# A graph network on one core: row-tiled second table, even edge loads, a wider record row, block numbers turned by PE, a fourth buffer for hop chunks

## What is computed

```python
# layer 0: basis message, self term, rows normalised
agg = segment_sum(h[src] @ W_msg + b_msg, dst);  out = agg + h @ W_self + b_self;  x += out / max(norm(out), 1e-12)
# layer 1: one of 16 relation matrices per edge
x += segment_sum(h[src] @ W_rel[edge_type], dst)
# layer 2: three hops over the weighted adjacency
emb = acc = h
for _ in range(3):
    emb = segment_sum(edge_weight[:, None] * emb[src], dst);  acc = acc + emb
x += acc / 4
# layer 3: an edge network with a gate
hidden = leaky(leaky(concat(xs[src], xt[dst], edge_attr @ We.T + be) @ W1.T + b1) @ W2.T + b2)
x += segment_sum(relu(hidden @ W3.T + b3) * xs[src], dst) + xt
```

## Time and profile before

| what | us |
|---|---|
| median of three runs | 8440.53 |
| the profiled execution | 8453.61 |
| its span | 8451.6 |
| PE busy | 5784.8 |
| DVE busy | 4682.9 |
| POOL busy | 4978.6 |
| ACT busy | 1528.8 |

### The profile page before, as it was taken

How to read it: one execution, slowest core, us unless ns; L and a number is a source line. 1 busy time by engine, 2 the same in 40 slices (tenths; PEclk the granted TensorE clock), 3 DMA queues, 4 the chain that set the end, 5 groups by cost and what they waited for, 6 DMA issues and landing times.

```text
span 8451.6 us, 133532 instructions
## 1 busy us (share of the span) xinstructions
PE 5784.8 (68%) x42197; PEld 4230.0 (50%) x42197; DVE 4682.9 (55%) x10280; ACT 1528.8 (18%) x4330; POOL 4978.6 (59%) x5265
## 2 busy tenths in 40 slices
PE   2476777777776555556554477777767788778877
PEld 2466666666644555555554222222235555555555
DVE  3688898998863667667664200000025555555555
ACT  1111111111122111111110000000013333333333
POOL 0577777777733777777777411111117777777776
PEclk6566556555555666666665699999976656665666
DMA  5655555555543444444442599999953333333332
GB/s 135 97 92 89 89 93 91 92 93 89 90 101 106 71 68 71 68 69 69 68 71 42 201 426 401 423 426 397 426 217 87 82 82 82 81 82 82 82 81 69
DMA packets 794607, 1178.96 MB, mean 139 GB/s; under 512 B 619664, under 2 KB 647729, under 8 KB 766544
## 3 DMA queue, kind: packets, MB, share of 16 engines
q1 hardware_dynamic: 616460, 919.49, 35.5%
q0 software_dynamic: 172528, 250.20, 16.2%
q10 hardware_dynamic: 5204, 4.11, 0.2%
HBM read 921.76 MB, written 258.23 MB: 140 GB/s over the span
## 4 chain that ended last, share of the span: by engine, by line
POOL 45%; issue 20%; DMA 16%; PE 12%; DVE 5%; ACTq 1%; DVEq 1%; POOLq 0%; ACT 0%; SPq 0%
POOL arena L497 44%; DMA arena<-B_d 12%; PE ps L931 5%; DMA arena<-tab,idx 2%; PE ps L842 2%; PE ps L884 2%; DVE ps L1228 1%; ACTq L279 1%; DMA arena<-rec_d,tcol 1%; DVE arena L1231 1%; DVE pair L1204 1%; PE ps L871 1%; PE ps L835 1%; DVE arena L1229 1%; POOL recb L506 1%
## 5 line engine op out<-in xcount | busy, mean ns | idle before, releaser
L497 POOL DMA_INDIRECT arena<-tab,idx x4992 | 4730.9, 948 | 1907.9 <-issue 1644.1
L884 PE MATMUL ps<-arena 128*128 128x64 f32 x6656 | 1351.6, 388 | 1088.0 <-DMA arena<-tab,idx 1010.2
L884 PEld LDWEIGHTS ps<-arena 128*128 128x128 f32 x6656 | 1288.0, 297 | 1172.0 <-issue 921.0
L871 PE MATMUL ps<-arena 128*64 128x98 f32 x15872 | 1368.0, 349 | 447.0 <-DVE arena L1231 440.3
L871 PEld LDWEIGHTS ps<-arena 128*64 128x64 f32 x15872 | 1152.4, 206 | 610.8 <-DVE arena L1231 548.0
L931 PE MATMUL ps<-arena,ev 128*64 128x512 f32 (+1 forms) x4836 | 1106.7, 603 | 370.8 <-DMA arena<-B_d 294.9
L1229 DVE TENSOR_TENSOR arena<-arena,ps 128x784 f32<-128x784 f32 x992 | 957.1, 965 | 0.0
L931 PEld LDWEIGHTS ps<-arena,ev 128*64 128x64 f32 x4836 | 383.9, 143 | 1093.3 <-issue 742.4
L534 POOL DMA_INDIRECT ev<-emb_d,dvI x186 | 175.1, 941 | 1259.5 <-PE ps L931 1041.4
L1190 DVE TENSOR_TENSOR arena<-relT,ps 128x1024 f32<-128x1024 f32 x624 | 759.3, 1217 | 201.7 <-issue 198.8
L1296 DVE COPY pair<-ps 128x512 f32<-128x512 f32 x9 | 5.7, 684 | 1437.4 <-PE ps L931 1437.4
(11 more groups left out here) (213 smaller groups left out, 3889.2 us busy)
## 6 DMA issues: line engine op xcount, KB each, us to landing
arena<-B_d SPq DMA_DIRECT2D x186, 3136.0 KB, 17.2
B_d<-stg SPq DMA_DIRECT2D x248, 784.0 KB
arena<-tab,idx POOLq DMA_INDIRECT x4992
arena<-rel_d SPq DMA_DIRECT2D x208, 256.0 KB
tab<-arena SPq DMA_DIRECT2D x26, 1024.0 KB, 3.8
attr_s<-arena SPq DMA_DIRECT2D x13, 512.0 KB, 14.6
stg<-attr_s SPq DMA_DIRECT2D x208, 32.0 KB
emb_d<-pair SPq DMA_DIRECT2D x3, 1664.0 KB, 16.3
```

The lines of the kernel that those rows point to most:

```text
L497: pool.indirect_dma_start(gat[:, r, k * width:(k + 1) * width], None, table, bass.IndirectOffsetOnAxis(ap=idx[:, r, k:k + 1], axis=0)).the ...
L871: ins = pe.matmul(ps[3 + j % 2][a * KP:(a + 1) * KP, i2 * KC:(i2 + 1) * KC], Lw[:, j % 2, t, :], Rc[:, j % 2, t, :], start=True, stop=True)
L884: ins = pe.matmul(ps[6 + r % 2][:, k * D:(k + 1) * D], S[:, r % 2, k, :], gat[:, r, k * D:(k + 1) * D], start=True, stop=True)
```

## The change

- `load_edges` splits its first transfer into 112 rows and 11 rows; the counts that are waited for rise to match.
- A row of rec_d has its 1024 attribute words first and then the fields; RW1 is 400 words in place of 385, so a row has 5696 bytes in place of 5636. The added words are zeroed.
- blk_d goes: the block numbers (blkw, one per partition) are multiplied with the identity by PE, into one row of ps4, and DVE copies that row into blkR in each turn. SP's 128x1 writes and the load at the end go.
- BUFS is 4. The tiles stg, recb, HS and HT move into the arena, which the hop chunks use as well. The embedding is written by ACT's queue at the start of each hop in place of SP's.
- In `project(1)` WR is loaded twice, on partitions 0 to 63 and 64 to 127. HS holds blocks without the 65th column, two blocks of 64 columns are transposed at once (128x128), and the products of two blocks, one on rows 0 to 63 and one on rows 64 to 127, follow each other for each half of 512 columns. New semaphores half_ps and half_mv release the first halves.
- In pass 0 the second of the three parts of a group gets its Lw from ACT (`weight_part`: eight ACTIVATE copies, 128x64 each, with the weight as scale) and no longer from DVE.

```diff
@@ load_edges
+        EVEN = FULL // 16 * 16
-            eng.dma_start(view[0:FULL], a[0:FULL * STEPS].rearrange("(p c j) -> p c j", c=NC, j=P)).then_inc(semaphore, 16)
+            for p0, p1 in ((0, EVEN), (EVEN, FULL)):
+                eng.dma_start(view[p0:p1], a[p0 * STEPS:p1 * STEPS].rearrange("(p c j) -> p c j", c=NC, j=P)).then_inc(semaphore, 16)
@@ sizes
-    RW1 = 3 * P + 1
+    RW1 = -(-(3 * P + 1) // 16) * 16
-    BUFS = 3
+    BUFS = 4
@@ sync: column turns
                 sp.dma_start(rel_d[bass.ds(c * P, P), :], fld16[h]).then_inc(stair_o[h], 16)
-                sp.dma_start(blk_d[bass.ds(c * P, P)].rearrange("(p u) -> p u", u=1), blki[:, h:h + 1]).then_inc(stair_o[h], 16)
@@ sync and scalar: hops
-                    if c == BUFS:
-                        sp.wait_ge(s_["emb_ok"], m + 2)
-                        sp.dma_start(emb_d.rearrange("(p b) f -> p (b f)", p=P), AG[:]).then_inc(s_["emb_out"], 16)
+                act.wait_ge(s_["emb_ok"], m + 2)
+                act.dma_start(emb_d.rearrange("(p b) f -> p (b f)", p=P), AG[:]).then_inc(s_["emb_out"], 16)
@@ scalar: project(1), move_pair
-                        for b in (2 * u, 2 * u + 1):
-                            if not has_nodes(j, b):
-                                continue
-                            act.wait_ge(s_["proj_ps"], (n * NJ + j) * BG + b + 1)
-                            for w in range(2):
-                                ins = act.copy(TO[:, b * NREL * D + w * 512:b * NREL * D + (w + 1) * 512], ps[2 + 2 * (b % 2) + w][:])
-                            ins.then_inc(s_["proj_mv"], blocks_done(j, b))
+                        for w in range(2):
+                            if w == 0:
+                                act.wait_ge(s_["half_ps"], j * 2 + (u + 1))
+                            else:
+                                act.wait_ge(s_["proj_ps"], (n * NJ + j) * BG + 2 * u + 2)
+                            for b in pair_of:
+                                ins = act.copy(TO[:, b * NREL * D + w * 512:b * NREL * D + (w + 1) * 512], ps[2 + 2 * (b % 2) + w][:])
+                            if w == 0:
+                                ins.then_inc(s_["half_mv"], 1)
@@ tensor: project(1), products
+                            for w0 in range(0, width, 512):
+                                if w0 == 0:
+                                    wait(pe, s_["half_mv"], j * 2 + u)
+                                else:
+                                    pe.wait_ge(s_["proj_mv"], (n * NJ + j) * BG + 2 * u)
+                                for b in pair_of:
+                                    t = b % 2
+                                    ins = pe.matmul(ps[2 + 2 * t + w0 // 512][:], HT[t * D:(t + 1) * D, q, u * P:(u + 1) * P],
+                                                    w[t * D:(t + 1) * D, w0:w0 + 512], start=True, stop=True)
@@ scalar: pass 0
+            def weight_part(c, h, j):
+                u = c * SUBS + j
+                ohp = ps[2 + 3 * (j % 2)][:].rearrange("p (s k) -> p s k", s=G)
+                act.wait_ge(s_["ohp_ok"], u + 1)
+                for k in range(G):
+                    at = 2 * P + j * G + k
+                    ins = act.activation(Lw[:, j % 2, k, :], ohp[:, k, :], ACT.Copy, scale=cols[:, h, at:at + 1])
+                ins.then_inc(s_["lhs_a"], 1)
@@ vector: pass 0, matrix_part
+                if by_scalar(n, t):
+                    dve.tensor_tensor(Rc[:, j % 2, :, :], column(1, KC), iota_view(0, KC), ALU.is_equal)
+                    dve.tensor_tensor(ohp, column(0, KP), iota_view(0, KP), ALU.is_equal).then_inc(s_["ohp_ok"], 1)
+                    return
@@ tensor and vector: column turns
+                pe.matmul(ps[4][0:1, 3 * P:4 * P], blkw[:], ident[:], start=True, stop=True).then_inc(s_["stair_T"], 1)
+                dve.tensor_copy(blkR[0:1, bass.ds(c * P, P)], ps[4][0:1, 3 * P:4 * P])
```

More of the change, by code:

```diff
@@ L322, in next_chunk, with by_scalar, weighted @@
             return None
+        def by_scalar(n, t):
+            return n == 0 and t == 1
+        def weighted(n, g, t):
+            if by_scalar(n, t):
+                return s_["lhs_a"], g + 1
+            if n == 0:
+                return s_["lhs_ok"], g * 2 + (1 + (t > 1))
+            return s_["lhs_ok"], g * PER_TURN[1] + (NG * 2 + t + 1)
         def column_turns(eng, body):
@@ L401, in _ @@
             for h in range(2):
-                sp.wait_ge(stair_o[h], 32 * (NC // 2 + 2 - h))
-            sp.dma_start(blkR[:], blk_d.rearrange("(u s) -> u s", u=1)).then_inc(s_["blk_in"], 16)
-            for h in range(2):
+                sp.wait_ge(stair_o[h], 16 * (NC // 2 + 2 - h))
                 sp.wait_ge(attr_o[h], 16 * (NC // 2 + 2 - h))
@@ L683, in groups @@
                             act.copy(idx[:, r, :], table[:, bass.ds((i * R + (R + r)) * G, G)]).then_inc(s_["idx_ok"], 1)
-                        for c, pos, h in parts[r]:
+                        for t, (c, pos, h) in enumerate(parts[r]):
+                            if by_scalar(n, t + 1):
+                                later = parts[r][t + 1]
+                                weight_part(later[0], later[2], later[1])
                             matrix_part(c, pos)
@@ L828, in products @@
                     pe.wait_ge(s_["ht_ok"], n * NJ + j + 1)
+                    if n == 1:
+                        for u in range(BG // 2):
+                            pair_of = [b for b in (2 * u, 2 * u + 1) if has_nodes(j, b)]
+                            if not pair_of:
+                                continue
+                            for w0 in range(0, width, 512):
+                                if w0 == 0:
+                                    wait(pe, s_["half_mv"], j * 2 + u)
+                                else:
+                                    pe.wait_ge(s_["proj_mv"], (n * NJ + j) * BG + 2 * u)
[3 more added lines that the diff above has]
+                                                    w[t * D:(t + 1) * D, w0:w0 + 512], start=True, stop=True)
+                                    if w0 + 512 >= width:
+                                        ins.then_inc(s_["proj_ps"], blocks_done(j, b))
+                                if w0 == 0:
+                                    ins.then_inc(s_["half_ps"], 1)
+                        return
                     for b in range(BG):
@@ L835, in products @@
                             ins = pe.matmul(ps[bank][:, c0:c0 + width], HT[0:k, q, b * P:(b + 1) * P], w[0:k, :], start=True, stop=True)
-                        elif not has_nodes(j, b):
-                            continue
-                        else:
-                            wait(pe, s_["proj_mv"], (n * NJ + j) * BG + b - 1)
-                            for w0 in range(0, width, 512):
-                                ins = pe.matmul(ps[2 + 2 * (b % 2) + w0 // 512][:], HT[0:k, q, b * P:(b + 1) * P], w[0:k, w0:w0 + 512],
-                                                start=True, stop=True)
-                        ins.then_inc(s_["proj_ps"], blocks_done(j, b) if width > 256 else 1)
+                            ins.then_inc(s_["proj_ps"], 1)
                 turn(0, 0)
```

97 lines of the change are left out of this document (55 added, 42 removed).

## The result

The changed kernel takes 8240.56 us (median of four runs, 8240.38 to 8245.69), the kernel before 8440.78 beside it: a ratio of 0.9763 (95% interval 0.9746 to 0.978), 200 us less. The profiled execution has a span of 8238.9 us.

| stage, from and to | before | after | moved | predicted |
|---|---|---|---|---|
| setup, to PE's first column turn | 166.9 | 112.2 | -54.7 | -57 |
| column turns, to the first gather of pass 0 | 120.5 | 62.5 | -58.0 | -45 |
| pass 0, first to last gather | 2125.9 | 2126.4 | +0.5 | 0 |
| second table, to the first gather of pass 1 | 222.1 | 133.3 | -88.8 | -76 |
| pass 1 | 2104.2 | 2104.4 | +0.2 | 0 |

A forecast was written before the change was run, and what follows sets the result against it. POOL's row gathers were taken to bound some 6300 of 8451.6 us, untouched. Setup 57, column turns 45, second table 76 and hops 22 sum to 200, giving 8240 us by the median; forecast's own range 8212 to 8268, overall 8185 to 8312.

The forecast's parts named there:

- Setup: Start of the kernel: splitting the 123-row loads starts DVE earlier and ends its wait for the root; -57 us, range -41 to -61.
- the 0 to 20 given: Setup: delay of the first table's writes by attribute copies and record arrays still going out; 0 to 20 us, +4 taken.
- Column turns: Thirteen turns before pass 0: dropping the four-byte blk_d writes ends stalled gathers, 9.0 to 5.5 us a turn; -45 us.
- the floor of 5.0: Column turns: shortest turn expected, from 4.2 us between transposes plus 0.8 for the added matmul and copy; bound of -52 us.
- The argument from the 392-byte writes: Column turns: pass 0 writes B_d in 392-byte pieces and keeps POOL's pace, so smallness of a few hundred bytes alone did not stall.
- Second table: Between the passes: block pairs on both row halves take one product's time, 15.0 to 7.55 us a turn; -76 us.
- the 1.53 estimated: Second table: pairing gain scaled from the Trainium skill to two row tiles, a turn of some 9.9 us, -52 instead of -76.
- Hops: Three hops: fourth buffer fills 7.6 us of idle DMA per change, write on ACT's queue some 3; -22 us.
- the lower bound's mechanism: Hops: the fourth load delays the embedding's write by its own 7.6 us, leaving a gain of 8 us.
- The upper bound, 34: Hops: gain if all idle DMA time between hops goes, 34 us.
- Passes: Gather passes: POOL's issues set the pace and no edit touches it, so nothing moves; 0 to -3 us.
- rival C: Pass 0: ACT's eight scaled copies stand in PE's way between groups, making the kernel slower, 8519 us; chance 0.04.

The follow-up runs named there:

- the second profile: The kernel before, unchanged, profiled once more: 8443.57 us, span 8444.8, with 111.3 us of column turns where the first profiled execution had 120.5.

## Why the prediction came out

*Setup, right.* DVE began at 13.62 (13.9 worked out; the loads were issued from 2.72 on and ran at 230 GB/s, not 177, so that so close an agreement is in part luck), the root came 64.65 us sooner (61), and the first table's writes ran into the record traffic, which cost 10 us (43.4 from the first write to the first column turn against 33.4), within the 0 to 20 given but more than the 4 taken. That nothing of the gain is there without the split loads is shown. The record pitch, which the prediction put at 0, is not nothing: with rows of 5636 bytes the stage took 8 us more.

*Column turns, right in the cause, and the size depends on the execution.* A turn takes 4.8 us on average, most of them 4.7 to 4.95, under the floor of 5.0 that was worked out, so the 0.8 for the added matmul and copy was a little too much. The gain is 58 us against the profiled execution, 49 against the second profile, and 46 when only the writes change (108.5 to 62.5). The prediction carried the 13 us between profile and median through as a constant; 9 of them were this stage's, and the changed kernel's profile has no such gap. The argument from the 392-byte writes stood, but the size of the words was not the reason: the Trainium skill's bound of 512 bytes ("DMA: Bandwidth & Descriptors", table of specifications) would have put the remaining 256-byte writes and the spread words in the same class as the neighbouring words, and neither stalls anything here (62.5 and 64.2 us). Side by side within 512 bytes they do.

*Second table, right in the mechanism, too small.* A pair takes as long as one product, as forecast: at a clock of 0.50 a record costs 0.44 us on both halves, 0.876 on one (0.878 in the run on half the rows), 1.98 times. That is above the 1.53 estimated from the Trainium skill's part on packing small matmuls ("TensorE: Matmul & The Clock Gate", Part 3). What the forecast lacked was the clock, which it held at 0.50, with a risen one as its upper bound, 6.1 us a turn and -91: the clock went to 1.00, the turns to 6.3 us and the stage to -88.8, with ACT and the table's writes as the new bound. Against the 7.55 of the forecast that is 1.3 us a turn, 13 in 10.25 turns, which is the difference. At 1.00 the pairs gain less: an unpaired record would take 0.44 there (an estimate, 0.876 halved) against 0.26, 1.7 times.

*Hops, the step that failed.* The fourth buffer filled idle DMA time (a share of 1.01 ahead of the gather and 0.48 behind it, where 5268:5282 had 0.17 before), but the write did not land 3 us sooner by sharing the engines. It did share them, and got 1.70 of 6.04 MB in 14 us, the rest going to chunks asked for ahead of it; it landed 0.2 us sooner. At the first hop, priced at a gain of 1, it lost 5.5: the fourth chunk, asked for 26 us earlier with the other three, was ahead of it, and with three buffers the loss is gone (41.6 against 42.0 before). That was the lower bound's mechanism, priced at 8 us in all; 11.2 were measured (16.7 less 5.5). The upper bound, 34, does not follow from the idle time that the term names: two changes of 11.6 are 23.

*Passes and rival C, right.* 0.218 us a copy, far under the 0.46 from which it would have counted.

The total owes something to chance. Between the profiles, 26 us too much gained in two stages stand against 2 too little in the setup and 11 in the hops; the remaining 13 are those by which the first profile stood above its median. So a clock that was left out (13) and a write that was priced too well (11) nearly cancel. The stages test the reasoning better than the total.

## What to carry to other kernels

Small writes are not dear by their size alone: 128 words side by side in one 512-byte stretch held up the gathers behind them (14.1 us to landing in place of 4.8), and spread out 512 bytes apart or turned into a row on PE they cost next to nothing. Where transfers bound a stage, what is asked for first decides: a deeper prefetch fills idle time and at the same time stands in front of the one small write that everything waits for, so that write belongs ahead of the last chunks. A matrix engine that is busy all the time on half its rows can have more than a factor of two left: here pairing on both halves gave 1.98, and the clock rose on top.

## What the runs showed of the hardware

- The granted clock stayed at 0.50 (1.2 GHz) with PE busy 158.08 of 160.00 us on 64 rows. With both halves in use it was 0.50 in 2359:2363 and 1.00 (2.4 GHz) in 2366:2420, with PE's products busy 35.82 of 54.00. No run tells whether the rows in use or the pace of the records makes the difference.
- Two products on rows 0 to 63 and 64 to 127, into different banks, took 0.44 us a record at a clock of 0.50; products on rows 0 to 63 alone took 0.878.
- Loads over 123 partitions ran at 62 GB/s, over 112 and 11 at 230. The Trainium skill, "DMA: Bandwidth & Descriptors", on the number of engines that a transfer is spread over, takes the largest number up to 16 that divides the outer size: 3 for 123, 16 for 112, 11 for 11. Three of 16 engines would be a share of 0.19 (an estimate from that rule); the DMA shares of 0.22 and 1.14 agree with it.
- 128 four-byte writes landed in 13.1 us side by side, in 1.8 us 512 bytes apart.
- A 1664-KB write needed 16.4 us to the gather behind it with four chunk loads requested ahead of it, 15.2 with three, and 9.1 with two.
- In one profiled execution with record rows of 5636 bytes a small write beside the attribute copies took 17 us to land, with 5696 less than 9 (31.34 to 40.19).
